# Wavelet stage of a two-block metaformer kernel: another order of the products, later restoring, twelve input buffers, a copy moved for every second chunk

## The reference

```python
x = x + _L0_conv_ref(_ln_c(x), ...)       # _ln_c: (v - mean) / sqrt(var + 1e-6) over the 64 channels
# _L0_conv_ref: Haar transform of 2 x 2 points into ll, lh, hl, hh, each scaled by exp(s_..)
low_proj = jnp.einsum('bchw,oc->bohw', subbands, w1) + b1
restored = jnp.einsum('bchw,oc->bohw', low_proj, w2) + b2      # then the inverse transform
t = _to_tokens(x)
t = t + _L0_ffn_ref(_ln_t(t), ...)        # gate logits of all tokens, the top 8 tokens of 32 experts
```

## Time and profile before

| what | us |
|---|---|
| median of three executions | 2098.15 (2095.51 to 2099.45) |
| the profiled execution | 2100.63 |
| its span, first to last instruction | 2098.8 |
| TensorE with a matmul under way | 1984.3 |
| VectorE busy | 1201.0 |
| ScalarE busy | 1035.5 |
| GpSimd busy | 592.4 |

### The profile page before, as it was taken

One profiled execution on the slowest core, in us unless ns is written; L12 is line 12 of the kernel. 1 busy time (PEld: TensorE's weight loads), 2 busy tenths in 40 slices (PEclk: granted clock), 3 DMA queues, 4 the chain that ended last, 5 costly groups with the idle time before them and its releaser, 6 DMA issues. The chain is left out here.

```text
span 2098.8 us, 41975 instructions
## 1 busy us (share of the span) xinstructions
PE 1984.3 (95%) x14926; PEld 1531.5 (73%) x14926; DVE 1201.0 (57%) x2548; ACT 1035.5 (49%) x2879; POOL 592.4 (28%) x686
## 2 busy tenths in 40 slices
PE   6999991699999989999999999999999799999998
PEld 3555550377777779999999999999999544444443
DVE  5888879566666653222222222232222399999998
ACT  4888874343444413333344444444444555555552
POOL 5888864222222200000000000000000455555551
PEclk9999995699999999999999999999999799999999
DMA  4955540222232200000000000000000356666653
GB/s 113 259 178 179 176 148 16 86 92 98 84 101 91 92 22 1 0 0 0 0 3 0 0 0 0 20 0 0 0 0 0 90 150 158 161 159 156 161 147 89
DMA packets 192679, 159.14 MB, mean 76 GB/s; under 512 B 25848, under 2 KB 159000, under 8 KB 192536
## 3 DMA queue, kind: packets, MB, share of 16 engines
q1 hardware_dynamic: 190840, 156.89, 26.7%
q0 software_dynamic: 512, 0.53, 0.1%
q10 hardware_dynamic: 1184, 0.00, 0.0%
HBM read 56.70 MB, written 67.11 MB: 59 GB/s over the span
## 5 line engine op out<-in xcount | busy, mean ns | idle before, releaser
L1228 PE MATMUL s_ps<-g_ring,g_T 128*128 128x128 f32 x7620 | 856.9, 275 | 7.9 <-DVE g_ring L1275 7.9
L1228 PEld LDWEIGHTS s_ps<-g_ring,g_T 128*128 128x128 f32 x7620 | 855.7, 192 | 8.7 <-DVE g_ring L1275 8.5
L1264 DVE SCALAR_TENSOR_TENSOR g_ring<-s_ps,s_xs 128x128 f32<-128x128 f32 x508 | 148.5, 292 | 421.3 <-PE s_ps L1228 421.2
L1327 ACT ACTIVATE g_X<-g_ring 128x256 f32<-128x256 f32 x254 | 172.2, 678 | 298.8 <-DVE g_ring L1264 298.8
L1707 DVE TENSOR_TENSOR tm_Z<-tm_pg,tm_nd 128x1024 f32<-128x1024 f32 x256 | 301.4, 1209 | 7.3 <-PE tm_pg L1547 6.1
L1561 PE MATMUL tm_po<-tm_Z,g_wexp 128*64 128x512 f32 x1024 | 249.0, 607 | 0.0
L1311 ACT ACTIVATE g_X<-g_ring 64x256 f32 x256 | 106.9, 418 | 203.4 <-DVE g_ring L1264 201.1
L1264 DVE SCALAR_TENSOR_TENSOR g_ring<-s_ps,g_X 128x128 f32<-128x128 f32 x254 | 74.0, 291 | 209.5 <-PE s_ps L1228 209.5
L1643 POOL TENSOR_TENSOR g_X<-g_x,g_X 128x512 f32<-128x512 f32 x64 | 82.9, 1298 | 350.9 <-POOLq L1204 287.5
L1350 POOL MEMSET g_zero<- 128x1 f32 x1 | 0.1, 98 | 577.1 <-POOLq L1204 577.1
L1322 ACT ACTIVATE s_xs<-g_X 128x256 f32<-128x256 f32 x254 | 161.2, 636 | 0.6 <-PEq L1204 0.6
(11 more groups left out here) (277 smaller groups left out, 3001.9 us busy)
## 6 DMA issues: line engine op xcount, KB each, us to landing
tm_nd<-g_X SPq DMA_DIRECT2D x256, 128.0 KB, 2.4
g_X<-in_x SPq DMA_DIRECT2D x128, 128.0 KB, 2.8
x1s<-g_X SPq DMA_DIRECT2D x64, 256.0 KB, 2.1
x1tok<-g_X SPq DMA_DIRECT2D x64, 256.0 KB, 2.4
g_x<-x2s SPq DMA_DIRECT2D x64, 256.0 KB, 2.9
y<-tm_yo SPq DMA_DIRECT2D x128, 128.0 KB, 2.5
g_X<-x1s SPq DMA_DIRECT2D x32, 256.0 KB, 2.8
x2s<-g_X SPq DMA_DIRECT2D x32, 256.0 KB, 2.0
```

The source lines that it names most:

```text
L1228: last = pe.matmul(out, g.T[i][:, d * P:d * P + P], g.ring[(u - 1) % RING][:, images(c), d:d + 64], start=(d == 0), stop=(d == ND - 1))
L1264: dve.scalar_tensor_tensor(g.ring[n % RING][:, images(c), inner], conv, 0.0, x[:, images(c)], ALU.max, ALU.add).then_inc(y_ready[c], 1)
L1327: act.activation(line(*place(n)), g.ring[n % RING][:, :, inner], ACT.Copy).then_inc(stored, 1)
```

## The change

- TensorE's order in a step is centre(c), variance(c - 1), token_centre(c - 5), low(c - 2), then in odd steps gate_logits and token_variance of the pair (c - 7) // 2, then turn(c - 4) and restore(c - 3). Token centring was behind the turning; restoring and turning are of a chunk one older; long steps are now the odd ones.
- ScalarE's order is square(c), the logarithm and the exponential of c - 1, token_square(c - 5), high_of_token(c - 4), in even steps copy_low(c - 2), in odd steps token_rstd.
- VectorE copies the low band in odd steps, behind normalise(c - 1) and ahead of copy_tokens. What it does with restored chunks and tokens is a step later.
- GpSimd's low_of_token is a step later, at the same place in its step.
- Twelve buffers for chunks instead of ten (ten semaphores for loads stay), four for token squares instead of two, LAG 7 instead of 5.

```diff
-    LAG = 5
+    LAG = 7
@@ TensorE
                 def low(c):
                     wait(pe, s["normed"], c + 1)
                     wait(pe, s["low_s"], c)
-                    wait(pe, s["tln"], (c - 3) // 2)
+                    wait(pe, s["tln"], (c - 4) // 2)
...
                         variance(c - 1)
+                    if now(c - 5):
+                        token_centre(c - 5)
                     if now(c - 2):
                         low(c - 2)
-                    if now(c - 5) and c % 2 == 0:
-                        gate_logits((c - 5) // 2)
-                        token_variance((c - 5) // 2, c - 2)
+                    if now(c - 6) and c % 2 == 1:
+                        gate_logits((c - 7) // 2)
+                        token_variance((c - 7) // 2, c - 2)
+                    if now(c - 4):
+                        turn(c - 4)
                     if now(c - 3):
-                        turn(c - 3)
-                    if now(c - 4):
-                        token_centre(c - 4)
-                    if now(c - 2):
-                        restore(c - 2)
+                        restore(c - 3)
@@ ScalarE
                         log_of_variance(c - 1)
-                    if now(c - 2):
-                        copy_low(c - 2)
                     if now(c - 1):
                         rstd(c - 1)
-                    if now(c - 3):
-                        high_of_token(c - 3)
-                    if now(c - 5) and c % 2 == 0:
-                        token_rstd((c - 5) // 2)
+                    if now(c - 5):
+                        token_square(c - 5)
                     if now(c - 4):
-                        token_square(c - 4)
+                        high_of_token(c - 4)
+                    if now(c - 2) and c % 2 == 0:
+                        copy_low(c - 2)
+                    if now(c - 6) and c % 2 == 1:
+                        token_rstd((c - 7) // 2)
@@ GpSimd
-                    if now(c - 3):
-                        low_of_token(c - 3)
+                    if now(c - 4):
+                        low_of_token(c - 4)
@@ VectorE
+                def copy_low(c):
+                    wait(dve, s["low_s"], c)
+                    wait(dve, s["low"], c + 1)
+                    wait(dve, s["rec"], c - 1)
+                    dve.tensor_scalar(lowS[c % 2], tv[:, 0:N // 2], g.b1[:], None, ALU.add).then_inc(s["low_s"], 1)
...
-                    if now(c - 3):
-                        add_restored(c - 3)
+                    if now(c - 4):
+                        add_restored(c - 4)
                     if now(c):
                         high_of_square(c)
                     if now(c + 2):
                         high_of_x(c + 2)
-                    if now(c - 6) and c % 2 == 1:
-                        scale_logits((c - 6) // 2)
-                    if c >= 8 and c % 2 == 0:
-                        block_top((c - 8) // 2)
+                    if now(c - 7) and c % 2 == 0:
+                        scale_logits((c - 8) // 2)
+                    if c >= 9 and c % 2 == 1:
+                        block_top((c - 9) // 2)
                     if now(c - 1):
                         normalise(c - 1)
-                    if now(c - 3):
-                        copy_tokens(c - 3)
+                    if now(c - 2) and c % 2 == 1:
+                        copy_low(c - 2)
+                    if now(c - 4):
+                        copy_tokens(c - 4)
```

More of the change, by code:

```diff
@@ L40 @@
 E0, HID, K0 = 32, 256, 8
-XBUFS = 10
+XBUFS, XSEMS = 12, 10
 AHEAD = 3
@@ L367, in load @@
                         sp.dma_start(buf(c)[t * C:t * C + C].rearrange("p (j w) -> p j w", j=JR),
-                                     x_chunk(a, c, t)).then_inc(xin[c % XBUFS], 16)
+                                     x_chunk(a, c, t)).then_inc(xin[c % XSEMS], 16)
                 def load_experts(q):
@@ L394, in _ @@
                         load_experts(c - 8)
-                    if now(c - 3):
-                        store_x1(c - 3)
                     if now(c - 4):
-                        store_tokens(c - 4)
+                        store_x1(c - 4)
+                    if now(c - 5):
+                        store_tokens(c - 5)
                 for u in range(XBUFS):
@@ L440, in token_variance @@
                     for half in range(2):
-                        last = pe.matmul(tv[half * C:half * C + C, :], g.J[:, C - E0:C + E0], tsq[half],
+                        last = pe.matmul(tv[half * C:half * C + C, :], g.J[:, C - E0:C + E0], tsq[(2 * pair + half) % 4],
                                          start=True, stop=True)
@@ L503, in copy_low @@
                         act.wait_ge(g.late_loaded, 16 * 6)
+                    wait(act, s["low_s"], c)
                     wait(act, s["low"], c + 1)
@@ L521, in token_square @@
                     wait(act, s["tcentred"], c + 1)
-                    wait(act, s["tvar"], c - 1)
-                    act.activation(tsq[c % 2], tc[:], ACT.Square).then_inc(s["tsquared"], 1)
+                    wait(act, s["tvar"], c // 2 * 2 - 2)
+                    act.activation(tsq[c % 4], tc[:], ACT.Square).then_inc(s["tsquared"], 1)
                 for c in steps:
@@ L572, in high_of_x @@
                 def high_of_x(c):
-                    wait(dve, xin[c % XBUFS], c // XBUFS * 32 + 32)
+                    wait(dve, xin[c % XSEMS], c // XSEMS * 32 + 32)
                     wait(dve, s["centred"], c - 1)
@@ L1797, in metaformer_kernel @@
         g.mix_loaded = m.sem("mix_loaded")
-        g.xin = m.sems("xin", XBUFS)
+        g.xin = m.sems("xin", XSEMS)
         g.taps_loaded, g.unit_ready, g.taps_turned, g.taps_hi, g.taps_cleared = (
@@ L1807, in metaformer_kernel @@
         g.xr = [v.take(N) for _ in range(XBUFS)]
-        g.sq, g.rr, g.nn, g.tsq = ([v.take(N) for _ in range(2)] for _ in range(4))
+        g.sq, g.rr, g.nn = ([v.take(N) for _ in range(2)] for _ in range(3))
+        g.tsq = [v.take(N) for _ in range(4)]
         g.lowS = [v.take(N // 2) for _ in range(2)]
```

## The result

The changed kernel takes 2145.78 us, median of four (2144.36 to 2149.42), against 2098.80 for the kernel before; the ratio is 1.0225 with a 95% interval of 1.0213 to 1.0238. It is slower by 47 us. The forecast was 2142, in a range of 2116 to 2160.

What follows compares the result with a forecast made beforehand. It held that queue order, not one engine's load, decides in the wavelet stage: 29 pairs x 1.46 = +42.3 us, drain +3.0, first steps -1.5, together +43.8 on 2098.15, giving 2142 us, range 2116 to 2160.

Steps and rivals of the forecast that it cites:

- The walk through a pair: Wavelet stage, one short and one long step: 10.33 us instead of 8.87, +1.46 a pair, 29 pairs, +42.3 us.
- The prices from rows: Operation times read from the earlier trace's rows, such as 0.23 us a 128x512 product; VectorE's new copy taken as 0.45.
- The ends: First steps and drain of the wavelet stage: -1.5 us and +3.0 us on the forecast.
- The start: First steps: restoring a step later no longer stands 0.64 us behind the low copy; -1.5 us, bounds 0 to -3.
- the drain: End of the stage: one more step drains the pipeline, +3.0 us, bounds 0 to 6.
- two waits in a row: TensorE in long steps: 1.35 us before token centring for GpSimd's low of token, 0.33 before token variance for VectorE's copy.
- Rival 2: Slower, but half: no first wait, the copy alone holds token variance, 0.7 us a pair, 2112 to 2126; chance 8%.
- Rival 1: Faster, 2093 us: TensorE sets the pace, 0.22 us a pair won; needs one GpSimd operation out of the chain; chance 8%.
- The second wait: Long step: token variance waits 0.33 us a pair for VectorE's low-band copy, delayed by a rounding that meets GpSimd.
- Rival 4: TensorE's idle time drops its clock to 1.2 GHz: up to 8 us more a pair, some 2330 us; chance 3%.

Runs made afterwards that it cites:

- e3: Changed kernel with token centring back behind the turning and every low-band copy on ScalarE, later restoring and twelve buffers kept; 2098.82 us, 0.9999 of the kernel before.
- e4: Changed kernel with GpSimd's low of token ahead of its low of x and VectorE's copy as changed; 2147.65 us, 1.0229 of the kernel before.
- e2: Changed kernel with every low-band copy on ScalarE and token centring as changed; 2142.87 us, 1.0200 of the kernel before.
- e9: On top of e4, GpSimd's low of x computed for only 256 of 512 columns in short steps; 2129.77 us, 1.0135 of the kernel before.
- e1: Changed kernel with token centring back behind the turning and VectorE's low-band copy kept in long steps; 2173.80 us, 1.0359 of the kernel before.
- e6: Changed kernel with token centring behind the turning, VectorE's copies moved to short steps and ScalarE's to long ones; 2098.54 us, 0.9992 of the kernel before.

## Why the prediction was right

The walk through a pair held link by link. Zero is L413 of the short step, 208.10 in the rows above:

| link | forecast | measured |
|---|---|---|
| rounding of the square, short step | 1.06 | 1.07 |
| low of token starts | 4.16 | 4.18 |
| low of token ends | 5.44 | 5.44 |
| token centring starts | 5.50 | 5.49 |
| low band starts | 6.06 | 6.15 |
| rounding of x, long step | 5.65 | 5.65 |
| VectorE's copy starts | 7.19 | 7.18 |
| token variance starts | 7.75 | 7.79 |
| next L413 of a short step | 10.33 | 10.39 |

The low band is late by the first token centring product, which takes 0.34 behind a wait (213.59 to 213.93) where 0.23 was put. That is hidden, because the copy is what token variance waits for. The 0.06 at the end are 0.04 at token variance, most of it the hand-over from VectorE (0.14 from the copy's end, 0.11 put), and 0.02 in what follows it. 29 x 1.52 = 44 us instead of 42.

The prices from rows were good: the new copy on VectorE took 0.47, 0.02 more than the 0.45 used and as long as ScalarE's in the earlier trace rows.

The ends were mis-sized. The start was to win 1.5 and won 0.1 by chunk 6 (41.86 instead of 41.95 us): the first steps did get shorter, 1.1 by chunk 3, but the step to chunk 6 gave it back. For the drain, the +7.2 above has to be taken apart. Of the 29 long steps that were counted, the one of chunk 63 lies behind the last centring product, so a part of the pairs' 44 us is in the 7.2. With 29 whole pairs taken off the time from chunk 6 to the end of the stage, 321.9 - 301.3 = 20.6 us are left in the changed kernel and 274.0 - 257.3 = 16.7 before: the drain is 3.9 longer, where 3.0 were put. It is 3.7 in e3, which has neither wait, so it does not come from the waits. Together 44.0 + 3.9 - 0.1, and 0.9 behind the stage, are the 48.7 us between the spans. Every term came out above its forecast, by 0.9 to 1.7; nothing cancelled, and the forecast is 4 us low against the median.

What was half wrong is the account of which wait matters. The prediction wrote 1.35 and 0.33 as two waits in a row. They are rows of one timeline, but their causes run beside each other: e4 takes away the first (1.32 as measured) and wins nothing, e2 takes away the second (0.27) and wins 0.25. The sum came out because the walk let token variance start at the later of the two. Rival 2 priced the copy alone at 0.7 a pair, with no long rounding, though the earlier trace rows show that the rounding is long when GpSimd is at work; e4 puts the copy alone at 10.41, 1.54 more than before, for there the rounding meets low of x instead. Rival 1 needed one GpSimd operation out of the chain; e4 took it out and shows that this was not the point that decided.

The second wait hangs on the long rounding. The Trainium skill (SBUF — State Buffer, section Who interferes with whom) tells of a lock that the engine which comes first holds for its whole instruction. The trace of e9 agrees: 0.54 us less of GpSimd and 0.54 less of the rounding. Behind GpSimd's end only 0.19 to 0.22 are left until the next operation, while an undisturbed rounding takes 0.34 to that point (209.17 to 209.51 in the changed kernel): part of it has passed before it stands still, and no run shows which.

Rival 4, the falling clock, did not come with the change: the stage keeps 1.00 behind idle stretches that the rows give as 1.15. It came in e1 behind 2.02. Its price rested on the early restoring of the earlier trace rows, 2.07 long; the table of stretches gives no lower granted clock there (1.00 for 27 to 30 us), so that this was the 1.2 GHz level is read from durations alone. e1 shows that level with its clock: restoring takes 1.91 in the stretch of 0.53, in place of 1.03.

## What to carry to other kernels

An operation moved to an engine with time to spare waits for all that stands ahead of it there, so look at what that queue does at the moment when the result is due, not at its busy share: the same copy on VectorE cost 75 us or nothing depending on the parity of the step (e1 and e6; some 15 of the 75 are the fallen clock), and beside the other wait it cost 3 (changed kernel and e2). Before an operation of a full engine is moved ahead, follow its input back to the last thing that its own step produces; the slack that it had is how far it can go. When two waits stand in one step, take away each alone and both together: two causes side by side look like one wait behind the other, and removing either shows little.

## What the hardware showed unexpectedly

In e1 TensorE's granted clock fell to the 1.2 GHz level behind idle stretches that the rows give as 2.02 us, in nine long steps, at 1.6 us each, and not in the others with the same stretch; behind 1.34 (e4) and 1.15 (changed kernel) no long step shows it. A rounding on VectorE that waits for GpSimd shows the wait as its own busy time (0.43 becomes 0.65 to 1.22 in the twelve traces), so VectorE looks busier than it is.
